# A fused attention and expert kernel: the row maxima computed thirteen rows ahead of the exponentials in place of sixteen

## The reference

```python
# layer 0: attention over 16 heads of 8 features, with a distance bias, then residual and norm
q, k, v = split(x @ qkv_w.T + qkv_b)
scores = einsum('bhid,bhjd->bhij', q, k) / sqrt(8) - |i - j| * 0.5 ** head
x = layernorm(x + softmax(scores) @ v @ out_w.T + out_b)
# layer 1: norm, attention over the two batch entries only, projection, norm,
# router over 8 experts, the best two of each token, GELU feed-forward of 512, sum
ln1 = ln(x); hidden = x + attention(ln1) @ proj_weight.T
probs = softmax(ln(hidden) @ router_weight); top_p, top_i = top_k(probs, 2)
out = layernorm(x + hidden + sum of the two experts' outputs, weighted by top_p)
```

## Time and profile before

| | |
|---|---|
| runs | 647.41, 649.9 and 653.12 us, median 649.9 us |
| profiled execution | 645.26 us, span 643.1 us from the first to the last instruction |
| mean granted TensorE clock | 0.903 |
| PE busy | 531.5 us (83%) |
| DVE busy | 398.0 us (62%) |
| ACT busy | 341.1 us (53%) |
| POOL busy | 215.4 us (33%) |

### The profile page before, as it was taken

The page is one execution under the profiler, slowest core; times in us unless marked ns, Lnnn a source line. Parts: engine busy times, 40 slices in busy tenths (PEclk is TensorE's granted clock), DMA queues, the critical chain, the costliest instruction groups (busy, mean ns, idle before and its releaser), DMA issues.

```text
span 643.1 us, 11439 instructions
## 1 busy us (share of the span) xinstructions
PE 531.5 (83%) x4355; PEld 286.8 (45%) x4355; DVE 398.0 (62%) x644; ACT 341.1 (53%) x662; POOL 215.4 (33%) x388
## 2 busy tenths in 40 slices
PE   6489999999999999999999989998813307999910
PEld 4224444444444545444544444453412206888700
DVE  2598777777986586988677798863073311322234
ACT  4137667677677676757777666865602101332304
POOL 4155613111143141047023124500415140545533
PEclk9679999999999999999999999997955557999975
DMA  7522332223222222222111212100001002443142
GB/s 175 154 92 78 76 116 82 85 87 109 78 81 92 78 92 76 77 73 68 55 39 49 88 58 72 52 3 14 30 8 33 1 17 63 140 128 86 57 137 65
DMA packets 47060, 47.60 MB, mean 74 GB/s; under 512 B 12800, under 2 KB 36770, under 8 KB 47009
## 3 DMA queue, kind: packets, MB, share of 16 engines
q1 hardware_dynamic: 41153, 34.30, 18.6%
q0 software_dynamic: 5312, 12.34, 6.0%
q10 hardware_dynamic: 544, 0.26, 0.2%
HBM read 31.87 MB, written 16.06 MB: 75 GB/s over the span
## 4 chain that ended last, share of the span: by engine, by line
PE 72%; DVE 16%; DMA 4%; ACT 3%; issue 3%; POOL 2%; SPq 0%; ACTq 0%; POOLq 0%; DVEq 0%
PE ps L753 32%; PE ps L791 16%; DVE row_max L1153 7%; PE ps L920 6%; PE ps L932 5%; PE ps L756 4%; PE ps L817 1%; PE ps L699 1%; DVE heads L1205 1%; PE ps L835 1%; DMA k_stacks<-k_dram 1%; PE ps L805 1%; DVE x_tok L1357 1%; DVE stats L1173 1%; PE ps L909 1%
## 5 line engine op out<-in xcount | busy, mean ns | idle before, releaser
L1153 DVE TENSOR_REDUCE row_max<-ps 128x1 f32<-128x1024 f32 x256 | 297.1, 1212 | 84.4 <-PE ps L756 42.1
L1012 ACT ACTIVATE probs<-ps 128x512 f32<-128x512 f32 x512 | 268.0, 605 | 92.5 <-PE ps L756 53.1
L753 PE MATMUL ps<-k_stacks,q_stacks 96*128 96x512 bf16 x512 | 165.4, 390 | 11.9 <-DMA k_stacks<-k_dram 5.6
L753 PE MATMUL ps<-q_stacks,k_stacks 99*128 99x512 bf16 x512 | 164.2, 383 | 4.1 <-ACT probs L1012 2.7
L791 PE MATMUL ps<-probs,v_unit 128*32 128x256 f32 x2048 | 125.3, 386 | 0.0
L756 PE MATMUL ps<-distance,slope_eye 128*128 128x128 bf16 x512 | 113.6, 222 | 0.0
L753 PEld LDWEIGHTS ps<-k_stacks,q_stacks 96*128 96x128 bf16 x512 | 43.9, 99 | 92.5 <-DVE row_max L1153 34.6
L791 PEld LDWEIGHTS ps<-probs,v_unit 128*32 128x32 f32 x2048 | 60.5, 110 | 54.5 <-issue 11.2
L753 PEld LDWEIGHTS ps<-q_stacks,k_stacks 99*128 99x128 bf16 x512 | 48.9, 98 | 57.5 <-ACT probs L1012 20.6
L756 PEld LDWEIGHTS ps<-distance,slope_eye 128*128 128x128 bf16 x512 | 50.4, 98 | 26.2 <-issue 2.8
L1080 ACT ACTIVATE probs<-ps 128x640 f32<-128x640 f32 x32 | 22.5, 705 | 67.8 <-PE ps L920 67.8
(11 more groups left out here) (174 smaller groups left out, 402.9 us busy)
## 6 DMA issues: line engine op xcount, KB each, us to landing
k_stacks<-k_dram SPq DMA_DIRECT2D x63, 144.0 KB
q_stacks<-q_dram SPq DMA_DIRECT2D x63, 72.0 KB
k_stacks<-in_c_alibi_k SPq DMA_DIRECT2D x32, 96.0 KB
w<-in_w SPq DMA_DIRECT2D x12, 256.0 KB, 2.9
xd<-blank POOLq DMA_DIRECT2D x8, 325.0 KB, 2.8
probs<-xd SPq DMA_DIRECT2D x8, 325.0 KB, 3.8
out_dram<-out_t SPq DMA_DIRECT2D x16, 128.0 KB
yt<-zeros POOLq DMA_DIRECT2D x4, 512.0 KB, 3.0
```

Source lines behind the costliest of these rows:

```text
L753: mm = pe.matmul(out, lhs, rhs, start=True, stop=not on_diagonal)
L1012: act.activation(probs[:, k % KEPT, HALF * e:HALF * (e + 1)], ps[:, n % RING, :], ACT.Exp).then_inc(ring_read, 1)
L1153: dve.tensor_reduce(row_max[:, m % 2, i:i + 1], max_pair(k).rearrange("p a n -> p (a n)"), AX.X, ALU.max).then_inc(mx_used, 1)
```

## The change

`LEAD` = 13 replaces the lead of two units. PE makes 13 max rows ahead of the first blocks; after that, max row NB·m + j + 13 goes with block row j of unit m. So the last three rows of unit m+1 go with j = 0, 1, 2 of unit m, and the first five of unit m+2 with j = 3 to 7. The wait for a unit's keys and queries moves to that unit's first max row. DVE takes the same order; it transposes a unit's maxima behind the second row of the next unit (`SWAP_BEHIND` = 1) where it was behind the third. On POOL `split_max(m + 1)` stands at the head of the loop over m in place of `split_max(m + 2)` at its end.

```diff
+ROWS = NB * UNITS
+LEAD = 13
+SWAP_BEHIND = 1
@@ POOL
             split_rest(5)
-            split_max(1)
             for m in range(UNITS):
+                if m + 1 < UNITS:
+                    split_max(m + 1)
                 for stage, c in hooks(2 * m):
                     late(stage, c)
...
                 for stage, c in hooks(2 * m + 1):
                     late(stage, c)
-                if m + 2 < UNITS:
-                    split_max(m + 2)
@@ PE
+            def max_row(k):
+
+                m, i = k // NB, k % NB
+                if i == 0:
+                    pe.wait_ge(loaded[m % SLOTS], 16 * loads_by(m))
+                for h in range(2):
+                    max_half(m, i, h)
@@
-            for m in range(2):
-                pe.wait_ge(loaded[m], 16 * loads_by(m))
-                for i in range(NB):
-                    if m == 0 and i == GROUP:
-                        pe.wait_ge(first_loaded, 32)
-                    if m == 0 and i == 1:
-                        pe.wait_ge(qf_ready, 4)
-                        pe.wait_ge(v_kept, 3)
-                    for h in range(2):
-                        max_half(m, i, h)
-                    if m == 0:
-                        first_work(i)
+            for k in range(LEAD):
+                if k == 1:
+                    pe.wait_ge(qf_ready, 4)
+                    pe.wait_ge(v_kept, 3)
+                if k == GROUP:
+                    pe.wait_ge(first_loaded, 32)
+                max_row(k)
+                first_work(k)
@@
                         if j == 0:
                             pe.wait_ge(max_loaded[m % SLOTS], 16 * turn_of(m))
-                            if m + 2 < UNITS:
-                                pe.wait_ge(loaded[(m + 2) % SLOTS], 16 * loads_by(m + 2))
-                        if m + 2 < UNITS:
-                            for h in range(2):
-                                max_half(m + 2, j, h)
+                        if NB * m + j + LEAD < ROWS:
+                            max_row(NB * m + j + LEAD)
@@ DVE
-            for m in range(-2, UNITS):
-                for i in range(NB):
-                    if m + 2 < UNITS:
-                        reduce_row(m + 2, i)
-                    if i == 2 and 0 <= m + 1 < UNITS:
-                        swap_max(m + 1)
-                    if i % GROUP == GROUP - 1 and m >= 0:
-                        for stage, c in hooks(2 * m + i // GROUP):
-                            late(stage, c)
+            for k in range(ROWS + LEAD):
+                if k < ROWS:
+                    reduce_row(k // NB, k % NB)
+                if k % NB == SWAP_BEHIND and NB <= k <= ROWS + SWAP_BEHIND:
+                    swap_max(k // NB - 1)
+                if k >= LEAD and (k - LEAD) % GROUP == GROUP - 1:
+                    for stage, c in hooks((k - LEAD) // GROUP):
+                        late(stage, c)
```

## The result

The changed kernel takes 668.42 us (median of 4 runs, 667.82 to 669.06) where the kernel before takes 650.43 us beside it (4 runs, 647.41 to 653.12). The ratio is 1.026, with a 95% interval from 1.0224 to 1.0296: slower by 18.0 us. The forecast was 666 us, with a range from 654 to 680. The profiled execution took 667.82 us, with a span of 665.6 us and a mean granted clock of 0.904.

The account below looks back on a forecast made before the run. The prediction took DVE to bound the start and PE the plain units. Its terms summed to +16.4 us, giving 666 us on the median 649.9, 2.5% slower, with a range from 654 to 680 for 8 in 10.

Parts of the forecast that it names:

- The start: Before the first blocks: PE's loop begins at 45.1 instead of 47.4 us, a gain of 2.3 us (2.0 to 2.7).
- The way of the maxima: Plain units: slack for writing and reading maxima falls from 2.3 to about 0.2 us; loads cost +2 us (0 to 8).
- 0.12 each: Flat cost in us taken per unit with expert fills, expert weights or the heads' load, for delaying the maxima's write.
- The transpose inside a group: Units 0 to 7 and 16 to 23: the transpose inside a group of four rows costs +0.8 us (0 to 1.4).
- `HID` behind the split: POOL's split waits for a later row, delaying `hid`, DVE and PE: +7.6 us in units 19, 27; +3.2 in 11, 14, 22.
- The clock: Units 19 and 27: the granted clock falls after PE's 3.7 us waits, slowing matmuls, +2.3 us each.
- The end: Unit 30: three max rows fall there, two hidden by PE's wait for ACT; +0.5 us (-1.7 to +1.2).
- The clock holding (661): Rival, chance 0.22: the clock stays at 2.4 GHz after PE's waits in units 19 and 27; 661 us.
- Late maxima in every unit (678): Rival, chance 0.17: write and read take longer, so PE waits in some 28 units; 674 to 688 us, say 678.
- The gain at the start prevailing (653): Rival, level 0.12, faster 0.03: `HID` doesn't bind, DVE's late statistics are made up in the `values`; about 653 us.
- start without gain: Rival, chance 0.04: something else, such as the slopes' load, bounds the start, so its gain is 0; 668 us.

## Why the prediction was right, and where its terms were off

**The start, -2.3: right, with 2.1.** The ledger's -2.4 owes its size in part to the scatter ahead of the tenth reduction: against the first trace of the kernel before, whose first unit comes at 48.58, it would be -1.3. Counted from the end of the tenth reduction the gain is 2.1 us in every pair of traces. PE went on at 46.05, not at 45.1, since that reduction ended 0.7 us later in this trace, and the read took 2.5 us to PE's start where 2.3 was taken.

**The way of the maxima, +2.0: too small, 5.4.** The step that failed is the flat "0.12 each" over 17 units. The slack of 0.2 us was right: unit 5's maxima are just in time. But the cost isn't spread. It sits in five units: 2.2 in unit 2, 0.9 in unit 3, 0.5, 1.3 and 0.4 in units 7, 9 and 12. PE's waits for the read are 2.00, 0.74, 0.27, 1.12 and 0.14 us there, 4.3 in all. Twelve units have fills of the buffers behind the experts, which I had counted first; nine of them cost nothing beyond the 0.15 of every unit. Unit 12 has the first of the larger fills (512 KB), and unit 9 has the load of the heads besides its fill. Units 17 and 25 have that load without a fill, and there the write took 1.46 and 1.69 us to the read's issue, where unit 9 has 3.06 here and 2.2 to 2.8 in the five other traces: it takes both, as far as this comparison goes; no run moved either. The sum lay inside the bounds of 0 to 8. That these are late maxima is shown for units 2, 3 and 9 by PE's waits for the read and by the transpose one row sooner, which takes them away; the load behind it is shown for unit 2 by moving `out_b` and for unit 3 by moving the weights. The size isn't fixed: the same five units cost 3.9 to 4.1 us in three other traces with the transpose in the same place, where unit 7 costs no more than a plain unit.

The Trainium skill (DMA: Bandwidth & Descriptors, section Anatomy of one DMA) gives a DMA of the GpSimd path a fixed cost of about 2.0 us. The writes on SyncE's queue landed after 1.5 us at the median here, and the quiet units show no wait of PE's matmuls for them, so the figure would have been too large for this queue, as the prediction had weighed it.

**The transpose inside a group, +0.8: about right in kind, small.** A plain unit costs 0.15. Two comparisons split it: 0.10 goes with the transpose's place (12.32 to 12.22), 0.05 with the lead of thirteen in place of fourteen (12.22 to 12.17). Over the remaining units that is 1.9 us, since nearly all have it and not only 14. That the 0.10 are DVE's gap at the transpose, as the prediction has it, no run shows by itself.

**`HID` behind the split, 2 x 3.8 and 3 x 1.1: right.** Units 11, 14 and 22 cost 1.09, 1.07 and 0.98. In unit 19 the forecast was a wait of 3.7 us, and it is 3.65. The chain is the one described: POOL's order unchanged, its first instruction waiting for a later row, DVE late by 4.12, PE by 3.65. Each link was cut by itself: the split behind the stages takes away all of it, the scatters behind `HID` take away exactly their 2.9.

**The clock, +2.3 each: right that it falls, too large.** It fell in both units, for 3.4 us, and costs 1.3 and 1.4. With the wait it makes 5.2 and 5.4 per unit where 6.1 were forecast. The `values` were nearly missed by the low level (2.25 in place of 1.93, not up to 3.64). But the size of the term isn't fixed: in two experiments the low level lasted 6.8 us and unit 19 took 18.7 and 18.9.

**The end, +0.5: -0.3.** PE's wait in unit 30 shrank to 1.45 us and the clock fell all the same (timeline of PE).

```profile
457.41 0.39 PE L755 MATMUL ps<-q_stacks,k_stacks 99*128 99x512 bf16 x1 [1.45 <-ACT probs L1015]
...
459.89 3.17 PE L801 MATMUL ps<-probs,v_unit 128*32 128x256 f32 x32
```

The low level lasted 3.4 us where it had lasted 6.8, so the `values` took 3.17 us in place of 3.64.

In sum +16.4 were forecast and +17.7 measured: 3.4 more for late maxima, 1.1 more for plain units, 1.7 less for units 19 and 27 with their clock, 0.8 less for the end, and half a microsecond less in units 0 and 1. So the mechanism was right, but that the forecast came within 2.4 us of the median is in part luck: misses of 4.5 us on one side met misses of 3.0 on the other.

**The rivals.** The clock holding (661) is refuted by the granted clock. Late maxima in every unit (678) are refuted by unit 5; late maxima in some are real. The gain at the start prevailing (653) needed DVE's delay to be made up in the `values`; PE's wait of 3.65 us says no, and so do the 1.0 to 1.1 us of units 11, 14 and 22. The fault "start without gain" is refuted by the 2.1 us of the start, though its 668 us are nearest to the measured 668.4; that is chance.

**What stays open.** Why the clock falls in unit 30 in some traces and not in others: PE waits there for ACT and then for `l`, 1.43 to 1.45 and 1.60 us. In two traces the clock fell for 3.4 us behind the first wait (the changed kernel and the one with `out_b` sooner), in two for 6.8 us behind the second, and in three it didn't fall (the split behind the stages, the scatters behind `HID`, the weights moved). And why one fall lasts 3.4 and another 6.8 us; what goes with it stands in the last section. The part behind the softmax was 182.4 to 182.9 us in four traces and 185.3 to 186.9 in the nine others. No edit moved it: the short ones are the first of the kernel before and all three that were taken beside the median of 647.12 us, the long ones were taken beside medians of 650.4 to 650.9. So but for that first trace it goes with the session, and what differs there isn't known.

## What to carry to other kernels

When rows of work are moved against each other, look at each wait whose instruction has not moved: an engine that works in order holds everything behind a wait, and a wait that had cost nothing for its event being long past can stop two other engines once the event is four rows later. Put such helpers behind the work of the same step that others wait for. A slack that is near zero is paid where large loads fall into the same stretch, not evenly, so list those loads one by one; and count a long wait of PE (2.4 us and more were followed by a low clock here) together with the slower matmuls behind it.

## What the hardware showed beyond that

- An 8 KB write on SyncE's queue was delayed by loads on POOL's: 1.47 us from its issue to the read's in quiet units, 2.35 to 2.6 with expert weights, 3.80 with a row spread over 128 partitions ahead of them.
- In eight traces PE waited 2.42 us or longer (up to 3.67) thirteen times between units 2 and 30, and each time the granted clock fell, from 0.8 us before to 1.1 us behind the wait's end. After the five waits of 1.8 to 2.2 us for the maxima of unit 3 it didn't fall. In the six cases in which the low level began 0.2 us or more ahead of the wait's end it lasted 6.8 us, in the seven others 3.4. So unit 19 took 18.7 us with the wait over at 301.27 and the clock low from 300.7 (`SWAP_BEHIND = 0`), and 17.3 with 308.31 and 308.9 (the changed kernel).
- The time that SyncE needs for one issue isn't constant: in the changed kernel the load of `q_stacks` at 121.37 us (line 346) took 1.23 us to issue, and the same line's at 146.12 us took 0.36.
